# A macaron transformer block on one core: rotary halves swapped by DMA, probabilities normalised by ScalarE and VectorE instead of GpSimd

## The chip, the cores and the metric

The kernel runs on one core of one Trainium2 chip. The metric is the device time of one execution in microseconds. Engines are named as in the profile: PE is TensorE (PEld its weight loads), DVE VectorE, ACT ScalarE, POOL GpSimd, SP SyncE. M is used below for the moment at which DVE begins the row maxima of a pair of heads.

## The reference, cut to what matters

The input is 16 sequences of 256 tokens of width 256, in float32. The block is x + 0.5 ffn(layernorm(x)), then x + attention(layernorm(x)), then x + 0.5 ffn(layernorm(x)), with a ternary feed-forward layer of 1024 hidden columns. The change touches only the attention:

```python
q = (x @ Wq).reshape(b, n, 16, 128).transpose(0, 2, 1, 3)   # 16 heads; k and v have 4
k = (x @ Wk).reshape(b, n, 4, 128).transpose(0, 2, 1, 3)
q = q * cos + rotate_half(q) * sin                          # rotate_half: (-t2, t1)
k = k * cos + rotate_half(k) * sin
scores = einsum('bhid,bhjd->bhij', q, repeat(k, 4)) * scale, masked above the diagonal
attn = softmax(scores)
out = einsum('bhij,bhjd->bhid', attn, repeat(v, 4)) * head_scale
return out.reshape(b, n, 2048) @ Wo
```

## The kernel before

Every float32 operand of a matrix product is cut into a float16 high part and a float16 low part, and a product is three matmuls (high by high, high by low, low by high).

The program has three stages, one after the other: a feed-forward layer over 8 tiles of 512 tokens, the attention over 16 batches (sequences), and the second feed-forward layer. In the attention each engine runs the same loop: batches b, and in a batch 8 pairs of query heads, i from 0 to 7. One turn of the loop is called a slot here. Pair t = 8b + i passes through the slots with a fixed lag, so that in one slot an engine works on several pairs. Before the change, in the slot of pair t:

- PE projects the queries of pair t (in the slots i = 0 and i = 4 the keys of two key heads come first), makes the scores of pair t-2, the values product of pair t-5, and two heads of the output projection of the batch before. In the slots i = 3 and i = 7 it also projects values.
- ACT copies the two halves of the projected 128 x 512 tile, swapped, from PSUM to SBUF (`rope_swap`, L474, two copies of 64 partitions), takes the exponentials of pair t-2 (L502, four activations with row sums), casts the normalised probabilities of pair t-3 to float16 (L509), scales the output of pair t-5 (L518), and casts the rotated tile to float16 (L525, L528).
- DVE takes the row maxima of pair t-2 with the mask (L944, four operations on PSUM), multiplies the projection by the cosines (L925, from PSUM) and the swapped halves by the sines (L925, from SBUF), makes the low part of the output (L955), the reciprocals of the row sums (L960) and the low part of the probabilities of pair t-3 (L964, one operation of 768 columns with two SBUF inputs).
- POOL adds the two rotary products (`rope_add`, L339), multiplies the exponentials of pair t-2 by the reciprocals (`norm`, L358, four pieces of 128 or 256 columns) and makes the low part of the rotated tile (`rope_lo`, L343).
- SP issues one DMA transpose of the probabilities of a pair (L268), once their low part is there.

In the slots with keys (i = 0 and 4) there is a second rotary tile, so that a batch has 10 rotary tiles for 8 pairs. Each rotary tile uses one of two projection banks and one of two buffers. At the edge of a batch the finished rows of the batch two before are added, normalised and turned (L987, L992, L995, L1000, L1006 on DVE, L348 and L350 on POOL).

The order on each engine is that of the program text, and the engines are joined by counting semaphores. The waits around the change are: `rope_mul` of tile r waits for the swap of r and for the add of r-2 (two buffers); `rope_add` waits for `mul`; the cast to float16 waits for `add`; `rope_lo` waits for that cast; `scores` waits for `rope_lo`.

Of the kernel before, what the change touches and what calls it, by code (L numbers as in the profile page):

```python
# [23 lines left out]
F32 = mybir.dt.float32  # L24
# [28 lines left out]
def program(nc, x, wq, wk, wv, wo, hscale, wu, wg, wd, cos_t, sin_t, out):  # L53
    ctx = ExitStack()
    with ctx:
# [38 lines left out]
        def pieces(lo, hi, dt, b):  # L94
# [8 lines left out]
        M1, M2, QK = pieces(0, 1024, F32, 2), pieces(1024, 2048, F32, 2), pieces(2048, 3072, F32, 2)  # L103
# [9 lines left out]
        COS = sb("COS", [P, 256], F32)  # L113
        SIN = sb("SIN", [P, 256], F32)
# [29 lines left out]
        RI = sb("RI", [P, 2, 4], F32)  # L144

# [23 lines left out]
        proj, swap, mul, add, qk_hi, qk_lo, v_hi, v_lo = (  # L169
            sem(n) for n in ("proj_done", "rope_swapped", "rope_mul", "rope_add", "qk_hi", "qk_lo", "v_hi", "v_lo"))  # L170
        s_done, mx, ex, rcp, pn = (
            sem(n) for n in ("scores_done", "max_done", "exp_done", "recip_done", "probs_normed"))
# [79 lines left out]
        def _(sp):  # L252
# [14 lines left out]
            def turn_probs(par):  # L267
                sp.dma_start_transpose(PT[:, par, :, :], PR[:, par, :]).then_inc(pt_t[par], 16)  # L268

            for e in range(2):  # L270
                sp.wait_ge(p_lo, e + 1)
                turn_probs(e)
            with sp.Fori(1, STEPS // 2) as m:
                for par in range(2):
                    ready, used = sp.to_reg(2 * m + par + 1), sp.to_reg(2 * m + par - 1)
# [3 lines left out]
                    turn_probs(par)  # L279
# [12 lines left out]
        def _(gp):  # L292
# [59 lines left out]
            def norm(e, par):  # L352

                wait_alone(gp, rcp, e + 1)
                for hh in range(2):
                    for blk, (lo, hi) in enumerate(BLOCKS):
                        c, lo, hi = 2 * hh + blk, 384 * hh + lo, 384 * hh + hi
                        last = gp.tensor_scalar(EX[:, par, lo:hi], EX[:, par, lo:hi], RI[:, par, c:c + 1], PS, ALU.mult, ALU.mult)  # L358
                last.then_inc(pn, 1)

            def batch(b):
                for i in range(PAIRS):
                    g, k = divmod(i, 4)
                    u, t = 2 * b + g, PAIRS * b + i
                    r, m = 5 * u + 1 + k, (5 * g + 1 + k) % 2
                    if real(b, i, 0):
                        if k == 0:
                            if isinstance(b, int) and b + i == 0:
                                gp.wait_ge(ff[0]["down_done"], FC * TILES - 2)
                            rope_add(r - 1, 1 - m)  # L370
                        if isinstance(b, int) and b + i == 0:
                            gp.wait_ge(ff[0]["down_done"], FC * TILES)
                        rope_add(r, m)
                    if real(b, i, 2):
                        norm(t - 2, i % 2)
                    if real(b, i, 0):
                        if k == 0:
                            rope_lo(r - 1, 1 - m, KH[:, g, :], KL[:, g, :])
                        rope_lo(r, m, QH[:, i % 2, :], QL[:, i % 2, :])
# [23 lines left out]
        def _(act):  # L403
            act.dma_start(HS[:, :], hscale).then_inc(hs_in, 16)
            act.dma_start(COS[:, :], cos_t).then_inc(tab_in, 16)
            act.dma_start(SIN[:, :], sin_t).then_inc(tab_in, 16)

# [648 lines left out]
```

## Time and profile before

| what | value |
|---|---|
| median of 3 runs | 1285.54 us |
| lowest, highest run | 1285.26, 1293.14 us |
| the profiled execution | 1293.14 us, its span 1293.1 us |
| busy in the span: PE, DVE, ACT, POOL | 1102.5, 1028.9, 883.7, 916.3 us |
| probability transposes (one a pair) | 128, the first at 272.1 us, the last at 1110.9 us |

The profile is one execution, the one that took 1293.14 us. Its page gives the busy time of each engine, the span cut in 40 equal slices, the chain of work that ended last, and the groups of instructions by line. An instruction's duration overlaps its follower's by some hundredths of a microsecond, so that what an instruction takes of its engine's time is the distance from its start to the next start.

### The profile page before, as it was taken

The page shows a single profiled execution, that of the slowest core. Times are in us where ns is not written, and L with a number is a line of the kernel's source. Part 1 is how long each engine was busy: PE and PEld are TensorE (multiplying, and loading weights), DVE is VectorE, ACT ScalarE, POOL GpSimd, SP SyncE. Part 2 cuts the span into 40 slices and gives each one's busy share as a digit, 9 for nine tenths or more (in the row PEclk, how much of TensorE's full clock was granted, in tenths as well). Part 3 has the DMA queues.
Part 4 walks back from the last instruction along what each step waited for, and adds up shares of the span by engine and source line. Part 5 has one row for each costly group of instructions (what it writes and reads, how often), then busy time and mean ns, then how long its engine had stood idle before and what let it go on. Part 6 is the DMA issues. An engine that isn't in the chain of part 4 may idle for free.

```text
span 1293.1 us, 29339 instructions
## 1 busy us (share of the span) xinstructions
PE 1102.5 (85%) x9152; PEld 838.9 (65%) x9152; DVE 1028.9 (80%) x2398; ACT 883.7 (68%) x2155; POOL 916.3 (71%) x1048
## 2 busy tenths in 40 slices
PE   3588899968888988888898888978988888899998
PEld 1254455657676777767777777767777777655555
DVE  3587788588899999999999999999999999533333
ACT  3264556578777877878788787877878777454444
POOL 1643545578888888888888888888888888344443
PEclk9799899989999999999999999999999999999999
DMA  8110000013333333332333333233333323200000
GB/s 317 31 52 1 1 0 0 1 38 63 62 50 62 61 61 61 57 64 51 59 61 61 61 61 58 52 61 60 61 61 61 61 49 67 44 17 32 16 32 32
DMA packets 214034, 67.82 MB, mean 52 GB/s; under 512 B 201200, under 2 KB 212720, under 8 KB 213744
## 3 DMA queue, kind: packets, MB, share of 16 engines
q1 hardware_dynamic: 213568, 67.13, 24.6%
q8 instruction: 18, 0.29, 0.1%
q10 hardware_dynamic: 432, 0.27, 0.1%
q14 instruction: 16, 0.13, 0.0%
HBM read 12.85 MB, written 4.19 MB: 13 GB/s over the span
## 4 chain that ended last, share of the span: by engine, by line
POOL 34%; issue 22%; DVE 12%; PE 9%; ACT 3%; POOLq 1%; DMA 0%; DVEq 0%; ACTq 0%; SPq 0%
POOL SCR L358 10%; POOL SCR L343 9%; POOL SCR L339 9%; PE bank L599 9%; DVE SCR L925 5%; POOL SCR L322 5%; DVE bank L944 2%; ACT SCR L474 1%; DVE ARENA L955 1%; POOL VE L348 1%; DVE ARENA L964 1%; DVE NM L944 1%; ACT SCR L502 0%; DMA SCR<-ARENA 0%; PE bank L570 0%
## 5 line engine op out<-in xcount | busy, mean ns | idle before, releaser
L358 POOL TENSOR_SCALAR SCR<-SCR,RI 128x128 f32<-128x128 f32 (+1 forms) x512 | 274.8, 537 | 42.8 <-DVE RI L960 2.6
L322 POOL TENSOR_TENSOR SCR<-SCR 128x512 f16<-128x512 f32 x128 | 150.6, 1177 | 196.1 <-ACT SCR L425 189.3
L339 POOL TENSOR_TENSOR SCR<-SCR 128x512 f32<-128x512 f32 x160 | 217.3, 1358 | 74.3 <-DVE SCR L925 72.4
L502 ACT ACTIVATE SCR<-bank,NM 128x128 f32<-128x128 f32 (+1 forms) x512 | 208.1, 418 | 60.6 <-DVE NM L944 58.6
L599 PE MATMUL bank<-SCR 128*128 128x128 f16 (+1 forms) x1536 | 159.7, 255 | 89.2 <-POOL SCR L343 80.9
L343 POOL TENSOR_TENSOR SCR<-SCR 128x512 f16<-128x512 f32 x160 | 213.9, 1346 | 10.8 <-ACT SCR L528 0.7
L425 ACT CAST SCR<-SCR 128x512 f16<-128x512 f32 x128 | 79.1, 618 | 178.7 <-DVE SCR L800 126.3
L800 DVE SCALAR_TENSOR_TENSOR SCR<-SCR,CS,bank 128x512 f32<-128x512 f32 x128 | 95.2, 744 | 128.8 <-PE bank L570 88.2
L964 DVE TENSOR_TENSOR ARENA<-SCR,ARENA 128x768 f16<-128x768 f32 x128 | 189.6, 1482 | 9.6 <-ACT ARENA L509 9.5
L599 PE MATMUL bank<-WOH,ARENA 128*128 128x256 f16 x1024 | 192.5, 276 | 2.6 <-DVE X L987 1.4
L599 PEld LDWEIGHTS bank<-SCR 128*128 128x128 f16 x1536 | 115.6, 101 | 121.4 <-issue 81.3
L474 ACT COPY SCR<-bank 64x512 f32<-64x512 f32 x320 | 185.5, 580 | 6.6 <-PE bank L599 0.8
L944 DVE CUSTOM_DVE_ANT_0 bank<-bank,MASK,SCQ 128x128 f32<-128x128 f32 (+1 forms) x512 | 183.5, 417 | 4.5 <-PE bank L599 1.7
L925 DVE TENSOR_TENSOR SCR<-SCR,SIN 128x512 f32<-128x512 f32 x160 | 167.3, 1046 | 0.0
L599 PE MATMUL bank<-SCR,ARENA 128*128 128x256 f16 (+1 forms) x1536 | 160.9, 259 | 4.3 <-DMA SCR<-ARENA 2.3
L528 ACT CAST SCR<-SCR 128x512 f16<-128x512 f32 x128 | 80.1, 626 | 112.7 <-POOL SCR L339 110.3
L599 PEld LDWEIGHTS bank<-SCR,ARENA 128*128 128x128 f16 x1536 | 133.0, 103 | 33.4 <-issue 16.9
L588 PE MATMUL bank<-TD,SCR 128*128 128x256 f16 x1024 | 133.8, 275 | 18.3 <-DVE TD L859 11.9
L925 DVE TENSOR_TENSOR SCR<-bank,COS 128x512 f32<-128x512 f32 x160 | 109.6, 685 | 42.2 <-ACT SCR L474 40.9
L599 PE MATMUL bank<-WOL,ARENA 128*128 128x256 f16 x512 | 141.4, 276 | 0.0
L588 PEld LDWEIGHTS bank<-TD,SCR 128*128 128x128 f16 x1024 | 99.9, 98 | 59.7 <-POOL SCR L322 18.1
L599 PEld LDWEIGHTS bank<-WOH,ARENA 128*128 128x128 f16 x1024 | 101.9, 99 | 16.5 <-DVE ARENA L955 2.1
(118 smaller groups left out, 2151.8 us busy)
## 6 DMA issues: line engine op xcount, KB each, us to landing
out<-X SPq DMA_DIRECT2D x7, 512.0 KB, 2.9
X<-in_x SPq DMA_DIRECT2D x1, 2560.0 KB, 10.0
ARENA<-in_wq SPq DMA_DIRECT2D x1, 2048.0 KB, 13.0
ARENA<-in_wo SPq DMA_DIRECT2D x1, 2048.0 KB, 18.2
SCR<-ARENA SPq DMA_TRANSPOSE x128, 3.7
X<-in_x SPq DMA_DIRECT2D x3, 512.0 KB, 9.7
X<-in_wu SPq DMA_DIRECT2D x1, 1024.0 KB, 7.0
X<-in_wg SPq DMA_DIRECT2D x1, 1024.0 KB, 8.8
```

Of the source, the lines that this page charges most:

```text
L322: gp.tensor_tensor(HL[:, f % 4, :], H32[:, f % 2, :], HH[:, f % 4, :], ALU.subtract).then_inc(s["hl_done"], 1)
L339: gp.tensor_tensor(QK[:, m, :], M1[:, m, :], M2[:, m, :], ALU.add).then_inc(add, 1)
L343: gp.tensor_tensor(lo, QK[:, m, :], hi, ALU.subtract).then_inc(qk_lo, 1)
L358: last = gp.tensor_scalar(EX[:, par, lo:hi], EX[:, par, lo:hi], RI[:, par, c:c + 1], PS, ALU.mult, ALU.mult)
L474: last = act.copy(M2[d:d + 64, m, :], PJ[m][s:s + 64, :])
L502: last = act.activation(EX[:, par, 384 * hh + lo:384 * hh + hi], SBK[hh][:, lo:hi], ACT.Exp, bias=NM[:, par, c:c + 1], scale=-1.0, accum_o ...
L588: last = pe.matmul(YB[sub // 2][:, (sub % 2) * D:(sub % 2 + 1) * D], hs[:, f % 4, sub * P:(sub + 1) * P], TD[:, f, :], start=f == 0 and a ...
L599: last = pe.matmul(dst, l(c), r(c), start=start and x == 0, stop=stop and x == len(todo) - 1, skip_group_check=True)
L800: ve.scalar_tensor_tensor(H32[:, f % 2, :], SG[:, f % 2, :], CS[:, 0:1], GB[f % 2][:, :], ALU.mult, ALU.mult).then_inc(s["h_done"], 1)
L925: last = ve.tensor_tensor(two(dst), two(src), tb[:, :].unsqueeze(1).to_broadcast([P, 2, SEQ]), ALU.mult)
L944: last = ve.tensor_tensor_reduce(SBK[hh][:, lo:hi], SBK[hh][:, lo:hi], MASK[:, 256 - (hi - lo):256], SCQ[:, 0:1], 3e38, ALU.add, ALU.min, ...
L964: ve.tensor_tensor(PR[:, par, 768:1536], EX[:, par, :], PR[:, par, 0:768], ALU.subtract).then_inc(p_lo, 1)
```

## The change

The projection tile is read once from PSUM by one DVE multiplication of 1024 columns, which writes both products, tile by cosines and tile by signed sines, to SBUF (MM). SP then moves the two halves of the sine product into each other's place with two DMAs from SBUF to SBUF (64 partitions by 512 float32 columns each, into MS), behind the wait for `mul` and in one queue with the transposes. POOL adds MM and MS. The add, the cast and the low part of a rotary tile move one slot later on POOL and ACT. ACT's two copies go.

POOL's four normalising multiplications go. ACT writes the normalised high part itself in four pieces (`act.mul` with the reciprocal as scale), one slot later than POOL normalised, ahead of the exponentials. DVE makes the low part in four pieces too, each a multiply by the reciprocal (a column pointer) and a subtraction. The reciprocal is taken in two DVE steps (RI0, then a multiply by 4096 into RI), with the low part of the output between them, and the first of them now stands ahead of that low part. The sines' sign is moved in the host's table.

```diff
+            def swap_halves(r, m):
+                wait(sp, mul, r + 1)
+                for d, s in ((0, 64), (64, 0)):
+                    sp.dma_start(MS[d:d + 64, m, :], MM[s:s + 64, m, 1, :]).then_inc(swapped[m], 16)
+
+            def batch(b):                                   # SP
+                for i in range(PAIRS):
+                    g, k = divmod(i, 4)
+                    r, m = 10 * b + 5 * g + 1 + k, (5 * g + 1 + k) % 2
+                    if real(b, i, 0):
+                        if k == 0:
+                            swap_halves(r - 1, 1 - m)
+                        swap_halves(r, m)
+                    if real(b, i, 3):
+                        turn_probs(PAIRS * b + i - 3, (i - 3) % 2)
...
-            def rope_add(r, m):
+            def rope_add(r, m, nth):                        # POOL, one slot later
                 wait(gp, qk_lo, r - 1)
-                gp.wait_ge(mul, r + 1)
-                gp.tensor_tensor(QK[:, m, :], M1[:, m, :], M2[:, m, :], ALU.add).then_inc(add, 1)
+                gp.wait_ge(swapped[m], 32 * nth)
+                gp.tensor_tensor(QK[:, m, :], MM[:, m, 0, :], MS[:, m, :], ALU.add).then_inc(add, 1)
...
-            def norm(e, par):
-                wait_alone(gp, rcp, e + 1)
-                for hh in range(2):
-                    for blk, (lo, hi) in enumerate(BLOCKS):
-                        c, lo, hi = 2 * hh + blk, 384 * hh + lo, 384 * hh + hi
-                        last = gp.tensor_scalar(EX[:, par, lo:hi], EX[:, par, lo:hi], RI[:, par, c:c + 1], PS, ALU.mult, ALU.mult)
-                last.then_inc(pn, 1)
...
-            def rope_swap(r, m):                            # ACT
-                wait(act, add, r - 1)
-                for d, s in ((0, 64), (64, 0)):
-                    last = act.copy(M2[d:d + 64, m, :], PJ[m][s:s + 64, :])
-                last.then_inc(swap, 1)
...
+                    if real(b, i, 3):                       # ACT, ahead of the exponentials
+                        e, par = t - 3, (i - 3) % 2
+                        act.wait_ge(rcp, e + 1)
+                        wait(act, pt_t[par], 16 * (4 * b + (i - 3) // 2))
+                        for hh in range(2):
+                            for blk, (lo, hi) in enumerate(BLOCKS):
+                                c, cols = 2 * hh + blk, slice(384 * hh + lo, 384 * hh + hi)
+                                last = act.mul(PR[:, par, cols], EX[:, par, cols], RI[:, par, c:c + 1])
+                        last.then_inc(p_hi, 1)
...
+                    if real(b, i, 1):                       # ACT, straight behind the exponentials
...
+                        act.wait_ge(add, r + 1)
+                        wait(act, s_done, 2 * (t - 1) - 2)
+                        act.copy(QH[:, j % 2, :], QK[:, m, :]).then_inc(qk_hi, 1)
...
-                ve.wait_ge(swap, r + 1)                     # DVE, rope_mul
-                two = lambda a: a.rearrange("p (h n) -> p h n", h=2)
-                for dst, src, tb in ((M1[:, m, :], PJ[m][:, :], COS), (M2[:, m, :], M2[:, m, :], SIN)):
-                    last = ve.tensor_tensor(two(dst), two(src), tb[:, :].unsqueeze(1).to_broadcast([P, 2, SEQ]), ALU.mult)
-                last.then_inc(mul, 1)
+                ve.wait_ge(proj, done)
+                two = PJ[m][:, :].rearrange("p (h n) -> p h n", h=2)
+                ve.tensor_tensor(MM[:, m, :, :].rearrange("p k (h n) -> p k h n", h=2),
+                                 two.unsqueeze(1).to_broadcast([P, 2, 2, SEQ]),
+                                 CS_TAB[:, :, :].unsqueeze(2).to_broadcast([P, 2, 2, SEQ]), ALU.mult).then_inc(mul, 1)
...
+                    if real(b, i, 2):                       # DVE, behind rope_mul of pair t
+                        ve.wait_ge(ex, 2 * e + 2)
+                        ve.reciprocal(RI0[:, :], RS[:, par, :]).then_inc(rcp0, 1)
                     if real(b, i, 6):
...
                     if real(b, i, 2):
-                        ve.wait_ge(ex, 2 * e + 2)
-                        wait(ve, pn, e - 1)
-                        ve.reciprocal(RI[:, par, :], RS[:, par, :]).then_inc(rcp, 1)
+                        ve.wait_ge(rcp0, e + 1)
+                        ve.tensor_scalar(RI[:, par, :], RI0[:, :], PS, None, ALU.mult).then_inc(rcp, 1)
                     if real(b, i, 3):
                         ve.wait_ge(p_hi, t - 2)
-                        ve.tensor_tensor(PR[:, par, 768:1536], EX[:, par, :], PR[:, par, 0:768], ALU.subtract).then_inc(p_lo, 1)
+                        for hh in range(2):
+                            for blk, (lo, hi) in enumerate(BLOCKS):
+                                c, cols = 2 * hh + blk, slice(384 * hh + lo, 384 * hh + hi)
+                                last = ve.scalar_tensor_tensor(PR[:, par, 768 + cols.start:768 + cols.stop], EX[:, par, cols],
+                                                               RI[:, par, c:c + 1], PR[:, par, cols], ALU.mult, ALU.subtract)
+                        last.then_inc(p_lo, 1)
```

## Rows read from the trace of the kernel before

**Rows 1.** The page: busy time of each engine, then tenths by slice.
```profile
PE 1102.5 (85%) x9152; PEld 838.9 (65%) x9152; DVE 1028.9 (80%) x2398; ACT 883.7 (68%) x2155; POOL 916.3 (71%) x1048
...
DVE  3587788588899999999999999999999999533333
```

**Rows 2.** Windows: us; PE, PEld, DVE, ACT, POOL busy; clock; DMA share; GB/s.
```profile
600.00:700.00 100.00, 86.90 (x809) 73.28 (x807) 93.33 (x226) 79.25 (x214) 85.38 (x103) 0.95 0.31 59
```

**Rows 3.** Timeline, POOL: the same step of two batches, one after the other.
```profile
578.12 0.78 POOL L348 TENSOR_SCALAR VE<-MV 128x2 f32<-128x2 f32 x1
...
631.30 0.78 POOL L348 TENSOR_SCALAR VE<-MV 128x2 f32<-128x2 f32 x1
```

**Rows 4.** Timeline of one slot, 600.43 to 605.71 us, all engines: start, us.
```profile
600.43 0.34 DVE L944 CUSTOM_DVE_ANT_0 bank<-bank,MASK,SCQ 128x128 f32<-128x128 f32 x1
...
601.45 0.37 ACT L502 ACTIVATE SCR<-bank,NM 128x128 f32<-128x128 f32 x1
...
601.78 0.68 DVE L925 TENSOR_TENSOR SCR<-bank,COS 128x512 f32<-128x512 f32 x1
...
602.04 2.71 POOL L343 TENSOR_TENSOR SCR<-SCR 128x512 f16<-128x512 f32 x2
...
602.38 1.36 DVE L925 TENSOR_TENSOR SCR<-SCR,SIN 128x512 f32<-128x512 f32 x1
...
603.04 0.84 ACT L509 CAST ARENA<-SCR 128x768 f16<-128x768 f32 x1
603.67 0.68 DVE L955 SCALAR_TENSOR_TENSOR ARENA<-bank,ARENA 128x512 f16<-128x512 f32 x1
...
604.27 0.16 DVE L960 RECIPROCAL RI<-RS 128x4 f32<-128x4 f32 x1
604.35 1.22 DVE L964 TENSOR_TENSOR ARENA<-SCR,ARENA 128x768 f16<-128x768 f32 x1
...
605.71 0.36 DVE L944 CUSTOM_DVE_ANT_0 bank<-bank,MASK,SCQ 128x128 f32<-128x128 f32 x1
```

**Rows 5.** By line, 500 to 1000 us: count, busy us, mean ns, idle before.
```profile
L964 DVE TENSOR_TENSOR ARENA<-SCR,ARENA 128x768 f16<-128x768 f32 x75 | 113.3, 1511 | 3.7 <-ACT ARENA L509 3.7
L925 DVE TENSOR_TENSOR SCR<-SCR,SIN 128x512 f32<-128x512 f32 x94 | 99.9, 1063 | 0.0
L528 ACT CAST SCR<-SCR 128x512 f16<-128x512 f32 x76 | 47.6, 626 | 64.2 <-POOL SCR L339 61.8 <-PE bank L599 2.4
```

**Rows 6.** One line each: count, duration in ns (least/median/most).
```profile
L925 DVE TENSOR_TENSOR SCR<-bank,COS x160: 674/684/693, 251.7 to 1092.6; 128x512 f32<-128x512 f32 x160
L925 DVE TENSOR_TENSOR SCR<-SCR,SIN x160: 670/927/1668, 252.3 to 1093.2; 128x512 f32<-128x512 f32 x160
L964 DVE TENSOR_TENSOR ARENA<-SCR,ARENA x128: 957/1535/2006, 270.4 to 1109.9; 128x768 f16<-128x768 f32 x128
L339 POOL TENSOR_TENSOR SCR<-SCR x160: 1257/1268/2088, 253.3 to 1094.8; 128x512 f32<-128x512 f32 x160
L343 POOL TENSOR_TENSOR SCR<-SCR x160: 1147/1158/1708, 256.5 to 1098.8; 128x512 f16<-128x512 f32 x160
```

**Rows 7.** The nearest to the new pieces: a column pointer, 256 columns.
```profile
L845 DVE SCALAR_TENSOR_TENSOR WKL<-SCR,AFAC,WKH x4: 485/485/485, 146.1 to 219.4; - x4
...
618.79 0.86 DVE L987 SCALAR_TENSOR_TENSOR X<-bank,CW,X 128x256 f32 x2
```

**Rows 8.** Timeline, 221 us: four short DVE operations against one of POOL.
```profile
221.12 2.23 DVE L770 TENSOR_SCALAR SCR<-X,MV,RSTD 128x256 f32 x4 [0.61 <-POOL RSTD L309]
...
221.24 1.32 POOL L322 TENSOR_TENSOR SCR<-SCR 128x512 f16<-128x512 f32 x1 [0.24 <-ACT SCR L425]
```

**Rows 9.** DMA issues: count, KB each, median us from issue to landing.
```profile
SCR<-ARENA SPq DMA_TRANSPOSE x128, 3.7
...
out<-X SPq DMA_DIRECT2D x2, 256.0 KB, 2.2
COS<-in_cos_t ACTq DMA_DIRECT2D x1, 128.0 KB, 3.9
```

More of the change, by code:

```diff
@@ L101, in program @@
         XN = pieces(6144, 7168, F32, 4)
-        M1, M2, QK = pieces(0, 1024, F32, 2), pieces(1024, 2048, F32, 2), pieces(2048, 3072, F32, 2)
+        MM = SCR[:, 0:2048].rearrange("p (m k n) -> p m k n", m=2, k=2)
+        QK = pieces(2048, 3072, F32, 2)
+        MS = sb("MS", [P, 2, 512], F32)
         QH, QL = pieces(3072, 3584, F16, 2), pieces(3584, 4096, F16, 2)
@@ L167, in program @@
         half_done, out_done = sem("last_sums_half_done"), sem("out_done")
[L169 to L172, printed above, removed]
+        proj, mul, add, qk_hi, qk_lo, v_hi, v_lo = (
+            sem(n) for n in ("proj_done", "rope_mul", "rope_add", "qk_hi", "qk_lo", "v_hi", "v_lo"))
+        swapped = [sem(f"rope_swapped{i}") for i in range(2)]
+        s_done, mx, ex, rcp0, rcp = (
+            sem(n) for n in ("scores_done", "max_done", "exp_done", "recip_done", "recip_scaled"))
         pt_t = [sem(f"probs_turned{i}") for i in range(2)]
@@ L265, in _, with turn_probs @@
             sp.dma_start(XV[:, 12:32, :], xv[:, 12:32, :]).then_inc(xin[3], 16)
[L267 to L275, printed above, removed]
+            def swap_halves(r, m):
+                wait(sp, mul, r + 1)
+                for d, s in ((0, 64), (64, 0)):
+                    sp.dma_start(MS[d:d + 64, m, :], MM[s:s + 64, m, 1, :]).then_inc(swapped[m], 16)
+            def turn_probs(e, par):
+                if not isinstance(e, int):
+                    ready, used = sp.to_reg(e + 1), sp.to_reg(e - 1)
                     sp.wait_ge(consts, 5)
@@ L278, in _ @@
                     sp.wait_ge(o_done, used)
-                    turn_probs(par)
+                else:
+                    sp.wait_ge(p_lo, e + 1)
+                    wait(sp, o_done, e - 1)
+                sp.dma_start_transpose(PT[:, par, :, :], PR[:, par, :]).then_inc(pt_t[par], 16)
+            def batch(b):
[8 more added lines that the diff above has]
+                        turn_probs(PAIRS * b + i - 3, (i - 3) % 2)
+            batches(sp, batch)
             with sp.Fori(0, TILES - 1) as n:
@@ L504, in batch @@
                             last.then_inc(ex, 1)
[L505 to L509 removed]
+                    if real(b, i, 1):
+                        j, unit = (i - 1) % PAIRS, 2 * b + (i - 1) // 4
+                        gj, kj = divmod(j, 4)
+                        r, m = 5 * unit + 1 + kj, (5 * gj + 1 + kj) % 2
+                        if kj == 0:
+                            act.wait_ge(add, r)
+                            wait(act, s_done, 8 * unit - 8)
+                            act.copy(KH[:, gj, :], QK[:, 1 - m, :]).then_inc(qk_hi, 1)
+                        act.wait_ge(add, r + 1)
+                        wait(act, s_done, 2 * (t - 1) - 2)
+                        act.copy(QH[:, j % 2, :], QK[:, m, :]).then_inc(qk_hi, 1)
                     if k == 3 and real(b, i, 0):
@@ L935, in batch @@
                     if k == 0 and real(b, i, 0):
-                        rope_mul(r - 1, 1 - m)
+                        if isinstance(b, int) and b + i == 0:
+                            ve.wait_ge(ff[0]["h_done"], FC * TILES)
+                        rope_mul(r - 1, 1 - m, 6 * u + 1)
                     if real(b, i, 2):
```

66 lines of the change are left out of this document (21 added, 45 removed).

## The prediction

> **What bounds the kernel now.** I read the page first. PE has the highest mean, but the slices show DVE at nine tenths from the ninth to the thirty-fourth, the whole attention [rows 1]. A window inside it gives DVE 93%, PE 87%, POOL 85%, ACT 79% [rows 2], so DVE comes first there and the others have room. The same step of two successive batches stands 53.2 us apart [rows 3]; 16 batches of this are some 850 us of the span, and the two feed-forward stages, about 440 us, are not touched.
>
> The timeline of one slot shows what fills DVE [rows 4]. From start to start: maxima 1.35 us, cosine multiply 0.60, sine multiply 1.29, output low part 0.60, reciprocal 0.08, probability low part 1.36, in all 5.28. The cosine multiply reads PSUM and always takes 0.67 to 0.69 us. The sine multiply has the same size with both inputs in SBUF and takes 0.67 at best, 1.67 at worst; the probability low part 0.96 to 2.01 [rows 6]. Both wait for POOL: at 602.38 the sine multiply starts while POOL's first L343 runs, and ends where 0.6 us of work behind the end of that POOL operation puts it [rows 4]. So an operation of DVE with two SBUF inputs and one of POOL exclude each other. By mean less best, over 10 tiles and 8 pairs, that costs DVE 0.39 x 10 + 0.55 x 8 = 8.3 us of the 53.2 [rows 5, 6]. The longest wait beside it is ACT's for POOL's add, 62 us in 500 [rows 5].
>
> The question is therefore not how much work leaves POOL and ACT, but what is left on DVE and where POOL's operations now fall.
>
> **Removed and added on DVE.** An instruction takes its columns over 0.96 per ns plus 0.07 us of DVE's time (512 columns in 0.60 [rows 4]). The wide multiply has 1024 columns from PSUM; it isn't in the trace, and by that line it takes 1.07 + 0.07 = 1.13 us, with two multiplies (1.20) as its upper bound. It takes the place of 0.60 plus a sine multiply of mean 0.98 (1.063 less the overlap of 0.08): 10 x 0.45 = 4.5 us a batch saved. No PSUM operation here waits for POOL, so it should not either.
>
> The probability low part of 768 columns takes 0.88 us when free (0.957 less 0.08) and becomes four pieces with a column pointer. The nearest rows have 256 columns: two from PSUM span 0.86 us, so 0.39 from start to start, and one from SBUF lasts 0.485, so 0.40 [rows 7]. That is 0.13 over the columns; a piece of 128 then takes 0.26, and the four 1.30. Bounds: 1.07 if the pointer cost nothing, 1.6 for four of 256. I take 1.30. The second reciprocal step adds 0.08 (0.3 if it has to wait for POOL as the short operations of rows 8 do).
>
> Here stands a rule of the Trainium skill, "VectorE: DVE Perf Modes", in its section on the TRN2 errata: a VectorE operation on SBUF pays 58 cycles plus one per column, and many small tiles pay the fixed part each time. By it the four pieces take 1.04 us, 0.26 less than my rows give, which over 128 pairs would be 33 us less; the fixed part of 0.13 us in rows 7 speaks against it.
>
> Without any exclusion the DVE work of a batch would be 8 x (1.35 + 1.13 + 0.08 + 0.60 + 0.08 + 1.30) = 36.3, plus 2 key tiles (2.3), 2 value low parts of the size of L955 (1.2) and the rows of the finished batch (eight operations of 256 columns by the same line and two of a few columns, about 3.0): 42.8 us, ten below 53.2. That is the gain on offer. The same count for the kernel before is 39.5 us: the change adds 3 us of work to the busiest engine and must win it back from exclusion.
>
> **Where POOL's operations fall.** POOL loses its four normalising pieces and keeps, a batch, 10 adds of 1.26 us and 10 low parts of 1.16 [rows 6], about 25 us against 45 now. DVE's exposed stretch is what has two SBUF inputs: the second reciprocal step and the four pieces, 1.4 us a slot. I lay out a slot from M, the start of the maxima.
>
> In the slot of rows 4 ACT's first exponential starts 1.02 us behind M and the cast behind the last at 2.6. DVE: maxima to 1.35, wide multiply to 2.48. The first reciprocal now stands right behind it and waits for the exponentials, so it starts at about 2.7 (the wait of 0.2 us is new, 1.6 us a batch; before, the sine multiply and the output low part covered it). Then output low part to 3.38, and there the exposed stretch wants to begin. ACT's next work behind the exponentials is the cast L528 (0.62 us), whose input, the add, has long been made: its multiply ended 3.2 us before M, and with 3 us for the swap (below) the add runs to 1.1 behind M. So the cast ends at about 3.15, and POOL's low part L343 runs from 3.2 to 4.35. Both follow from the same event, the end of the exponentials, one by 0.6 to 0.65 us and the other by 0.7 to 0.8. The low part therefore meets the exposed stretch in every slot and costs it 0.95 us: the stretch runs from 4.33 to 5.71. A regular slot takes 5.7 us; 8 of them 45.6, with key tiles, value low parts and rows 52.1.
>
> If POOL comes second it is no better, because four pieces can be broken into: at 221 us four DVE operations of 0.4 us began 0.12 us before a POOL operation, which took 1.32 instead of 1.16, so it had the port after the first of them, and the four took 2.23 us together [rows 8]. The one operation of 768 columns could not be interrupted like that. So each POOL operation that arrives in the stretch costs its whole length. In the slots behind the key tiles POOL makes two low parts back to back: 2 x 1.16 = 2.3 more, 54.4. In the key slots the add of the key tile waits for the regular low part and starts right behind it, in the pieces: 2 x 1.26 = 2.5 at most, and I take half, 1.3: 55.7. The adds of the query tiles come at swap landing, about 5.5 behind M, at the last piece; they count nothing here, and up to 4.9 in the range where the stretch is already late.
>
> **The swap.** Two DMAs of 128 KB on SP, behind `mul` and ahead of the transpose. The nearest rows land in 2.2 us (256 KB) and 3.9 (128 KB at the start, beside the other loads); a transpose lands in 3.7 [rows 9]. With two issues of 0.4 I take 3 us behind the multiply, bounds 2.2 and 6. The DMA share is 0.31 [rows 2], so there is room. Nothing but SP's own queue stands behind the wait: a transpose has two slots until PE wants it, and `mul` of the next pair follows the low part that the transpose waits for, so SP gets no new blocking. The add is wanted by the end of the exponentials, 5.7 us behind the multiply; with 1.3 for the add itself the swap has 4.4 us before anyone waits, and every microsecond beyond that moves cast and low part back by as much.
>
> ACT loses two copies (1.17 us a tile) and the cast of 0.84, and gains four pieces of roughly 1.4 us; POOL loses 2 us a pair. Neither was first, so both count nothing, as long as DVE paces the slot. PE is busy 87% of 53.2, 46 us a batch [rows 2], and isn't the bound either.
>
> **The sum.** 55.7 - 53.2 = 2.5 us a batch, 16 batches: +40 us on the profiled 1293.1, so 1333. That execution was 7.6 us over the median of the runs, so 1326 for the median: +3%.
>
> **Rivals.**
> (a) The operations don't line up, and POOL's 25 us fall evenly over the batch. The stretch then meets a running operation with 0.45 x 0.6 = 0.27 us and is broken into by 0.37 a us x 1.0 us x 1.2 = 0.45: 0.7 a slot instead of 0.95 and no extra for the keys. 42.8 + 1.6 + 8 x 0.7 + 0.5 = 50.5, or 43 us less: 1243. For it: the sine multiply's duration now spreads from 0.67 to 1.67 us [rows 6], so the phases do vary. Against: the two releases by one event.
> (b) Nearly no exclusion, as the change intends: 42.8 + 1.6 and some waits, say 47: 1185. It decides if the low parts run under the maxima, that is if the add is late by more than 3 us. PE's 46 us a batch would come next.
> (c) A column pointer costs nothing in SBUF, so that the pieces take 1.07 us by the line above, and everything else is as forecast: 55.7 - 8 x 0.23 = 53.9, +11 us: 1296, within 1%. For it: the line holds for all other operations of rows 4. Against: both rows of rows 7. The errata section of the Trainium skill's page "VectorE: DVE Perf Modes" gives 1.04 us for them, and with it 1292.
> (d) Every add also falls in the stretch, because a longer stretch catches more of them: 54.4 + 2.5 + 4.9 = 61.8, +138 us: 1423. A swap of 6 us instead of 3 has the same effect, since the add then lands at 2.5 behind M and the low part in mid-stretch.
>
> **Chances.** Forecast 0.42 (1305 to 1365), (d) or its half 0.20, (a) 0.18, (b) 0.07, (c) 0.13. A difference within 1% (13 us) is about what a measurement of this kernel can't tell from none. Slower by over 1%: the forecast and (d), 0.62. Same: (c), 0.13. Faster: (a) and (b), 0.25. The range leaves out (b) and the far end of (d): 1240 to 1395. The forecast's own range is 1305 to 1365.
>
> **What the profile would show.** Each right if: the wide multiply is 1.21 us and never longer (else the PSUM argument fails); batches stand 55 to 57 us apart by L348's place; the pieces have least durations of 0.34 and 0.47 and means well above them, most of the excess in whichever piece comes as L343 begins; the second reciprocal step has a mean far over its least of 0.15; POOL is under 60% busy and DVE over 90%; the swaps land in about 2.5 us. A low part that starts under the maxima, or pieces at their least duration, would make me wrong towards faster; a POOL add that waits for the swap while ACT waits for the add, with DVE idle, would mean that the transfer sets the time, not the exclusion.

## The result, and the profile after

The changed kernel takes 1369.0 us against 1286.0 for the kernel before: ratio 1.064, interval 1.061 to 1.067. The prediction had the sign, and its range of 1240 to 1395 holds the time; the forecast was +40 us, and +83 were measured. The profiled execution has a span of 1368.4 us, 75 more than before.

The page of the changed kernel: busy time of each engine, then DVE's tenths by slice, then the new DMAs (KB each, median us to landing).
```profile
PE 1127.5 (82%) x9152; PEld 871.5 (64%) x9152; DVE 1142.0 (83%) x2750; ACT 787.4 (58%) x2219; POOL 597.3 (44%) x536
...
DVE  3585887799999999999999999999999999743333
...
MS<-SCR SPq DMA_DIRECT2D x320, 128.0 KB, 2.3
SCR<-ARENA SPq DMA_TRANSPOSE x128, 3.6
```
Its window for 600 to 700 us, columns as in [rows 2]:
```profile
600.00:700.00 100.00, 80.48 (x725) 68.80 (x724) 97.06 (x243) 62.30 (x203) 45.95 (x40) 0.90 0.48 98
```
POOL fell from 85% to 46% in this window and ACT from 79% to 62%, while DVE rose from 93% to 97% [rows 2]. Two engines were relieved, and the one that paces the attention was not. The clock granted to TensorE was 0.90 here and 0.95 before, but that does not set the time: between 500 and 1000 us DVE waits for PE 3.4 us in all, and the normalising half alone (below) takes the same time at a mean granted clock of 0.95, against 0.93 for the whole change.

The timeline of POOL, the same step of two successive batches, answers to [rows 3]:
```profile
600.71 0.19 POOL L367 TENSOR_SCALAR VE<-MV 128x2 f32<-128x2 f32 x1 [2.52 <-DVE MV L1003]
...
658.72 0.19 POOL L367 TENSOR_SCALAR VE<-MV 128x2 f32<-128x2 f32 x1 [2.53 <-DVE MV L1003]
```
A batch takes 58.0 us instead of 53.2. Sixteen times 4.8 is 77 us, so the whole difference arises in the attention.

One line each, as in [rows 6] (count, duration in ns least/median/most): the wide multiply, the two steps of the reciprocal, the four pieces of the probability low part, and POOL's low part.
```profile
L921 DVE TENSOR_TENSOR SCR<-bank,CS_TAB x160: 1201/1211/1226, 253.3 to 1167.4; 128x1024 f32<-128x1024 f32 x160
L955 DVE RECIPROCAL RI<-RS x128: 166/178/180, 266.6 to 1182.1; 128x4 f32<-128x4 f32 x128
L963 DVE TENSOR_SCALAR RI<-RI x128: 158/1058/1066, 266.8 to 1182.8; 128x4 f32<-128x4 f32 x128
L970 DVE SCALAR_TENSOR_TENSOR ARENA<-SCR,RI,ARENA x512: 335/471/1556, 272.0 to 1186.3; 128x128 f16<-128x128 f32 x86, 128x256 f16<-128x256 f32 x85
L362 POOL TENSOR_TENSOR SCR<-SCR x160: 1144/1154/1335, 260.3 to 1176.2; 128x512 f16<-128x512 f32 x160
```
The wide multiply never takes over 1.226 us: it reads PSUM, and once started it does not wait for POOL. The second step of the reciprocal works on four columns, has a least duration of 0.158 us and a median of 1.058. POOL's low part lasts 1.15 at the median and 1.34 at most, where it went up to 1.71 before [rows 6]: when this low part and DVE's four-column step meet now, it is DVE that waits.

How they meet is in the timeline of a regular slot, all engines, which answers to [rows 4]:
```profile
615.00 0.34 DVE L943 CUSTOM_DVE_ANT_0 bank<-bank,MASK,SCQ 128x128 f32<-128x128 f32 x1
...
616.34 1.21 DVE L921 TENSOR_TENSOR SCR<-bank,CS_TAB 128x1024 f32<-128x1024 f32 x1
...
617.43 0.63 ACT L515 CAST SCR<-SCR 128x512 f16<-128x512 f32 x1
617.58 1.10 SPq L274 DMA_DIRECT2D MS<-SCR  x2
617.58 0.18 DVE L955 RECIPROCAL RI<-RS 128x4 f32<-128x4 f32 x1
...
617.68 0.66 DVE L959 SCALAR_TENSOR_TENSOR ARENA<-bank,ARENA 128x512 f16<-128x512 f32 x1
...
618.14 1.16 POOL L362 TENSOR_TENSOR SCR<-SCR 128x512 f16<-128x512 f32 x1 [2.24 <-ACT SCR L515]
618.26 1.06 DVE L963 TENSOR_SCALAR RI<-RI 128x4 f32<-128x4 f32 x1
...
619.23 1.39 DVE L970 SCALAR_TENSOR_TENSOR ARENA<-SCR,RI,ARENA 128x128 f16<-128x128 f32 x4
...
620.46 1.30 POOL L358 TENSOR_TENSOR SCR<-SCR,MS 128x512 f32<-128x512 f32 x1 [1.17 <-DMA MS<-SCR]
620.55 0.68 DVE L975 SCALAR_TENSOR_TENSOR ARENA<-bank,ARENA 128x512 f16<-128x512 f32 x1
```
ACT's cast follows the last exponential and ends at 618.06. POOL's low part starts at 618.14, and 0.12 us later DVE comes to L963, which ends with the low part. The four pieces behind it then run in 1.32 us, as if free. From 615.00 to the end of the pieces at 620.55 are 5.55 us; 5.7 was forecast. The halves' DMAs are issued at 617.58, and the add (L358) starts at 620.46, 2.9 us behind the end of its multiply and within the last piece, which it no longer delays.

Then come the slots with a key tile. First POOL's timeline, then DVE's, which shows the four pieces as one row:
```profile
625.42 1.15 POOL L362 TENSOR_TENSOR SCR<-SCR 128x512 f16<-128x512 f32 x1 [3.66 <-ACT SCR L515]
626.53 2.54 POOL L358 TENSOR_TENSOR SCR<-SCR,MS 128x512 f32<-128x512 f32 x2
633.41 2.27 POOL L362 TENSOR_TENSOR SCR<-SCR 128x512 f16<-128x512 f32 x2 [4.34 <-ACT SCR L512]
635.80 1.54 POOL L358 TENSOR_TENSOR SCR<-SCR,MS 128x512 f32<-128x512 f32 x1
```
```profile
625.54 1.06 DVE L963 TENSOR_SCALAR RI<-RI 128x4 f32<-128x4 f32 x1
626.51 3.50 DVE L970 SCALAR_TENSOR_TENSOR ARENA<-SCR,RI,ARENA 128x128 f16<-128x128 f32 x4
...
634.51 3.38 DVE L970 SCALAR_TENSOR_TENSOR ARENA<-SCR,RI,ARENA 128x128 f16<-128x128 f32 x4
```
At 626.5 the adds of the key tile and of the query tile run back to back and both fall into the pieces: 3.50 us instead of 1.39. In the next slot, at 634.5, it is the second low part and, behind the second piece, a whole query add: 3.38. In the slot of 600.5 us two more things happen: POOL, which had waited 2.52 us for DVE's row statistics (the first row of the batch distance above), is so late with its add that the wide multiply waits for the buffer, and the next add runs into the centring of the row:
```profile
603.05 1.23 DVE L921 TENSOR_TENSOR SCR<-bank,CS_TAB 128x1024 f32<-128x1024 f32 x1 [1.04 <-POOL SCR L358]
...
605.21 2.38 DVE L970 SCALAR_TENSOR_TENSOR ARENA<-SCR,RI,ARENA 128x128 f16<-128x128 f32 x4
607.51 1.68 DVE L1008 TENSOR_SCALAR SCR<-X,MV,RSTD 128x256 f32 x2
```

### The profile page after: what moved, and what is told of

Read it like the earlier page. It is cut to its first block, busy times and chain, and to the rows that moved or that the text cites. A ratio compares the mean times of both kernels' runs of the same rounds, so it can differ in the third digit from the quotient of the medians.

```text
span 1368.4 us, 29292 instructions
## 1 busy us (share of the span) xinstructions
PE 1127.5 (82%) x9152; PEld 871.5 (64%) x9152; DVE 1142.0 (83%) x2750; ACT 787.4 (58%) x2219; POOL 597.3 (44%) x536
## 4 chain that ended last, share of the span: by engine, by line
issue 24%; PE 20%; POOL 17%; DVE 13%; ACT 4%; DMA 3%; SPq 1%; POOLq 1%; DVEq 0%; ACTq 0%
PE bank L597 19%; POOL SCR L358 6%; POOL SCR L362 6%; POOL SCR L341 4%; DVE ARENA L970 4%; ACT SCR L502 3%; DMA MS<-SCR 3%; DVE bank L943 2%; DVE RI L963 2%; DVE SCR L921 2%; DVE ARENA L959 1%; DVE NM L943 1%; SPq L274 1%; DVE ST L1000 0%; DVE SCR L1008 0%
## 5 line engine op out<-in xcount | busy, mean ns | idle before, releaser
L362 POOL TENSOR_TENSOR SCR<-SCR 128x512 f16<-128x512 f32 x160 | 183.5, 1155 | 381.8 <-ACT SCR L515 310.1
L970 DVE SCALAR_TENSOR_TENSOR ARENA<-SCR,RI,ARENA 128x128 f16<-128x128 f32 (+1 forms) x512 | 264.5, 574 | 0.0
L358 POOL TENSOR_TENSOR SCR<-SCR,MS 128x512 f32<-128x512 f32 x160 | 211.3, 1329 | 97.8 <-DMA MS<-SCR 92.3
L341 POOL TENSOR_TENSOR SCR<-SCR 128x512 f16<-128x512 f32 x128 | 150.7, 1178 | 201.5 <-ACT SCR L434 193.8
L493 ACT ACTIVATE ARENA<-SCR,RI 128x128 f16<-128x128 f32 (+1 forms) x512 | 191.0, 444 | 63.7 <-DVE RI L963 60.1
L921 DVE TENSOR_TENSOR SCR<-bank,CS_TAB 128x1024 f32<-128x1024 f32 x160 | 194.0, 1213 | 15.3 <-POOL SCR L358 14.8
L434 ACT CAST SCR<-SCR 128x512 f16<-128x512 f32 x128 | 79.1, 618 | 179.7 <-DVE SCR L798 126.8
L597 PE MATMUL bank<-SCR,ARENA 128*128 128x256 f16 (+1 forms) x1536 | 178.3, 276 | 0.7 <-DMA SCR<-ARENA 0.6
L963 DVE TENSOR_SCALAR RI<-RI 128x4 f32<-128x4 f32 x128 | 121.3, 947 | 0.1
L428 ACT ACTIVATE SCR<-bank,SU 128x512 f32<-128x512 f32 x128 | 87.6, 684 | 31.2 <-PE bank L560 29.9
L502 ACT ACTIVATION_READ_ACCUMULATOR SCR<-bank,NM 128x1 f32 x512 | 103.8, 203 | 0.0
```

Source lines behind the costliest of these rows:

```text
L341: gp.tensor_tensor(HL[:, f % 4, :], H32[:, f % 2, :], HH[:, f % 4, :], ALU.subtract).then_inc(s["hl_done"], 1)
L358: gp.tensor_tensor(QK[:, m, :], MM[:, m, 0, :], MS[:, m, :], ALU.add).then_inc(add, 1)
L362: gp.tensor_tensor(lo, QK[:, m, :], hi, ALU.subtract).then_inc(qk_lo, 1)
L493: last = act.mul(PR[:, par, cols], EX[:, par, cols], RI[:, par, c:c + 1])
L502: last = act.activation(EX[:, par, 384 * hh + lo:384 * hh + hi], SBK[hh][:, lo:hi], ACT.Exp, bias=NM[:, par, c:c + 1], scale=-1.0, accum_o ...
L597: last = pe.matmul(dst, l(c), r(c), start=start and x == 0, stop=stop and x == len(todo) - 1, skip_group_check=True)
```

## The experiments

The theory after the result: the probability low part, split into pieces and led by a four-column step, stands at a fixed distance behind the end of the exponentials, and so does POOL's low part; they meet in every slot, and since the pieces can be broken into, POOL's further operations get in too. The rivals were that the transfer of the halves delays POOL (rotary half of the change), and that the added work on DVE alone is the price. The kernel before took 1284.3 us beside the first four kernels and 1293 to 1296 beside the others, so only ratios are compared. To be explained: 1.064.

**One piece in place of four.**
```
-  for hh in range(2):
-      for blk, (lo, hi) in enumerate(BLOCKS): ...
-          last = ve.scalar_tensor_tensor(PR[...low], EX[...], RI[:, par, c:c + 1], PR[:, par, cols], ALU.mult, ALU.subtract)
+  ve.tensor_tensor(PR[:, par, 768:1536], EX[:, par, :], PR[:, par, 0:768], ALU.subtract).then_inc(p_lo, 1)
```


> The changed kernel, but the low part of the probabilities is again one tensor_tensor of 768 columns (EX minus the high part; the multiply by the reciprocal is left out of the low part). Exclusion theory: the slots lose the 0.42 us that four pieces cost over one (8 x 0.42 = 3.4 us a batch), and POOL can no longer come in between pieces, so that most of the extra 1.0 to 2.1 us of the slots behind the keys goes as well (about 5 us a batch): batches of 50 us instead of 58, 1369 - 16 x 8 = about 1240 us, range 1225 to 1270. Rival (the pieces cost only their own fixed part): 1369 - 55 = about 1315. Rival (the swap's latency or PE sets the slot): no less than 1350.

This kernel leaves out the multiply by the reciprocal in the low part. It takes 1295.3 us, ratio 1.009 (1.008 to 1.011). By line, 500 to 1000 us:
```profile
L963 DVE TENSOR_SCALAR RI<-RI 128x4 f32<-128x4 f32 x75 | 73.2, 977 | 0.0
L967 DVE TENSOR_TENSOR ARENA<-SCR,ARENA 128x768 f16<-128x768 f32 x75 | 71.9, 959 | 0.0
L943 DVE CUSTOM_DVE_ANT_0 bank<-bank,MASK,SCQ 128x128 f32<-128x128 f32 x150 | 53.0, 353 | 30.8 <-PE bank L597 29.1
```
The four-column step still waits for POOL in nearly every slot (mean 0.977), but the single operation has its least duration, 0.959, on average: once it holds its place, nothing gets in. The batches fall from 58.0 to between 53.0 and 54.2 us, 53.5 in the mean, and 5.5 of the 6.4 points are gone. The work saved is 1.32 less 0.88 (0.96 less the overlap) = 0.44 us a pair, or 3.5 a batch. What got in between the pieces goes as well: their means in the changed kernel were 597 and 538 ns, 262 and 68 over the least for their size, which makes 5.3 a batch. Of these 8.8 only 4.5 show, for others came back: the maxima now wait 3.1 us a batch for PE's scores (0.4 in the changed kernel), and the two centring operations of the rows take 1.26 us each (0.88). That is why the time lies above the 1225 to 1270 expected.

**No transfer** (the exchange of the halves is left out).
```
-  sp.dma_start(MS[d:d + 64, m, :], MM[s:s + 64, m, 1, :]) ...   # and its calls
-  gp.wait_ge(swapped[m], 32 * nth); gp.tensor_tensor(QK[:, m, :], MM[:, m, 0, :], MS[:, m, :], ALU.add)
+  gp.wait_ge(mul, r + 1);           gp.tensor_tensor(QK[:, m, :], MM[:, m, 0, :], MM[:, m, 1, :], ALU.add)
```


> The changed kernel without the two swap DMAs; POOL adds the two products straight behind the multiply (the exchange of the halves is left out). Exclusion theory: the transfer is hidden, but the adds come about 3 us earlier, under the output low part and the exposed stretch: 1.0 us behind the multiply instead of 3, so they may meet the stretch in every slot; 1350 to 1440 us, not faster by more than 20 us. Rival (the transfer's latency is what made it slower): clearly faster, 1290 to 1320.

1430.9 us, ratio 1.115 (1.113 to 1.117): without its DMAs the kernel is 5 points slower. POOL's timeline, DVE's pieces in the same slot, and the pieces by line, 500 to 1000 us:
```profile
632.34 1.15 POOL L358 TENSOR_TENSOR SCR<-SCR 128x512 f16<-128x512 f32 x1 [4.66 <-ACT SCR L511]
633.45 1.27 POOL L354 TENSOR_TENSOR SCR<-SCR 128x512 f32<-128x512 f32 x1
```
```profile
633.43 2.49 DVE L966 SCALAR_TENSOR_TENSOR ARENA<-SCR,RI,ARENA 128x128 f16<-128x128 f32 x4
```
```profile
L966 DVE SCALAR_TENSOR_TENSOR ARENA<-SCR,RI,ARENA 128x128 f16<-128x128 f32 x130 | 104.6, 805 | 0.0
...
L966 DVE SCALAR_TENSOR_TENSOR ARENA<-SCR,RI,ARENA 128x256 f16<-128x256 f32 x130 | 86.8, 667 | 0.0
```
Without the wait for the landing, the add (L354 here) follows the low part (L358) back to back and falls into the pieces, which take 2.49 us here instead of 1.39. In the changed kernel the means were 597 and 538 (window 500 to 1000 us), so the pieces of an average slot take 0.67 us more; 128 slots of that are 86 us, of which 62 show in the time. That is rival (d) of the prediction, in the slots that the changed kernel had spared. The transfer was hidden, and its delay kept the query adds out of the pieces.

**The rotary half alone** (GpSimd normalises, as before, between its adds and its low part; one low part operation of 768 columns on DVE) and **the other half alone** (kernel before, with the normalising of the changed one):
```
rotary half, GpSimd:   add, add | + norm(PAIRS * b + i - 2, i % 2) | rope_lo, rope_lo
other half:            COS / SIN tables, rope_swap on ACT and two multiplies as before;
                       ACT's four act.mul, reciprocal in two steps and DVE's four pieces as in the change
```


> The rotary half of the change alone; POOL normalises as before, one low-part operation. Exclusion theory: POOL's work is as before (about 39 us a batch free of waits) and DVE loses its sine multiply with two SBUF inputs, 10 x 0.6; port time of both together falls from 39 + 14 = 53 us to 39 + 8 = 47 a batch, and DVE needs 40: 48 to 50 us a batch, 1200 to 1240 us. Rival (the transfers cost more than the copies they replace): 1285 or more.

> The normalising half alone, on the kernel before: pieces on ACT and DVE, rotary part by copies and two multiplies. Exclusion theory: DVE has 43.5 us a batch free of waits, and both the sine multiply and the interruptible stretch of 1.4 us a slot meet POOL's adds and low parts: 55 to 60 us a batch, 1310 to 1390 us. Rival (taking the four pieces off POOL is the gain, the rotary half the loss): 1200 to 1260 us.

The normalising half alone takes 1369.0 us, ratio 1.066 (1.064 to 1.068), the same as the whole change, with a batch of 57.9 us. It meets POOL at other places: the sine multiply is free (mean 675 ns), and the pieces wait.
```profile
L963 DVE SCALAR_TENSOR_TENSOR ARENA<-SCR,RI,ARENA 128x256 f16<-128x256 f32 x138 | 128.4, 930 | 0.0
```
The rotary half alone takes 1561.8, ratio 1.217 (1.215 to 1.219). That is far over the 1200 to 1240 expected, and falls among the "1285 or more" of the rival, the transfers, but the next run shows another cause. The waits of the rotary half, 500 to 1000 us (total, times, longest):
```profile
DVE bank L951 <- PE bank L605: 185.9, 58, 5.3
POOL SCR L377 <- DVE RI L969: 167.9, 57, 3.8
...
PE bank L605 <- POOL SCR L362: 137.3, 52, 3.6
```
It is a ring. POOL's normalising (L377) waits for DVE's reciprocal, the rotary low part (L362) stands behind it, PE's scores wait for that low part, and DVE's maxima wait for the scores. I put the normalising on the wrong side of the low part. The repair is to move it behind, and ACT's cast with it:
```
 rope_add; rope_add
-norm(PAIRS * b + i - 2, i % 2)
 rope_lo; rope_lo
+norm(PAIRS * b + i - 2, i % 2)
```


> The rotary half alone again, but POOL makes the low part of the rotated tile ahead of the normalising pieces instead of behind them, and ACT casts the rotated tile ahead of the probabilities. If the 1562 us came from a ring (low part behind normalising behind the reciprocal behind the exponentials, and the next scores behind the low part), it opens: 1200 to 1290 us. If the transfers or their waits made it slow, it stays above 1450.

1313.5 us, ratio 1.014 (1.012 to 1.017). The ring is open, with the transfers as they were, so 20 of the 22 points were the order. But 0.93 to 1.00 times the time before was not reached, and a part for the transfers is not excluded. In 500 us, DVE waits 56 for ACT's cast and PE 85 for the rotary low part; POOL is busy 79%. Why it isn't faster I have read only in part. So the rotary half, at this order, brings nothing by itself; its 0.45 us saved per multiply do not show.

**The low part of the query tiles cut to 64 of 512 columns.**
```
-  gp.tensor_tensor(lo, QK[:, m, :], hi, ALU.subtract) ...
+  gp.tensor_tensor(lo[:, 0:n], QK[:, m, 0:n], hi[:, 0:n], ALU.subtract) ...   # n: 64 for query tiles, 512 for key tiles
```


> The changed kernel, but POOL's low part of the query tiles has 64 of its 512 columns (the rest of the low parts is left out), so that it holds the port for about 0.2 us instead of 1.16. Exclusion theory: the scaled reciprocal no longer waits (its mean falls from 0.98 us to under 0.35), each slot gets 0.8 us shorter and the second low part behind the keys goes: about 8 us a batch, 1369 - 130 = 1240 us; where PE's wait for the low part sets the pace the floor is about 1200. Rival (pieces cost by their number, not by who holds the port): over 1340.

1217.9 us, ratio 0.940 (0.938 to 0.942), 12 points better for taking 0.85 us off an operation of an engine that is busy 46%. By line:
```profile
L970 DVE SCALAR_TENSOR_TENSOR ARENA<-SCR,RI,ARENA 128x256 f16<-128x256 f32 x165 | 78.1, 473 | 0.0
L970 DVE SCALAR_TENSOR_TENSOR ARENA<-SCR,RI,ARENA 128x128 f16<-128x128 f32 x164 | 69.4, 423 | 0.0
L963 DVE TENSOR_SCALAR RI<-RI 128x4 f32<-128x4 f32 x82 | 27.2, 332 | 0.0
L362 POOL TENSOR_TENSOR SCR<-SCR 128x64 f16<-128x64 f32 x82 | 25.2, 308 | 138.6 <-ACT SCR L515 138.6
```
The four-column step goes from 0.978 to 0.332, and the pieces of 256 to their free duration. By the means that is 0.65 us a slot for the step and 0.48 for the pieces, in all 9.0 a batch, and the two centring operations give 0.9 more (401 ns each instead of 876). The batches fell to between 48.0 and 49.4 us, by 9.6 in the mean. So POOL's low part costs DVE more than its own length (8 x 0.85 = 6.8).

**The second reciprocal step given to ACT.**
```
+act.wait_ge(rcp0, e + 1)
+act.mul(RI[:, par, :], RI0[:, :], PS).then_inc(rcp, 1)
-ve.tensor_scalar(RI[:, par, :], RI0[:, :], PS, None, ALU.mult).then_inc(rcp, 1)
```


> The changed kernel, but ACT makes the scaled reciprocal instead of DVE. It waited 0.9 us for the port in every slot. Exclusion theory: the first piece waits in its place and only the instruction's own 0.08 us goes, 10 us in all: 1350 to 1369. Rival (a short operation in the port's queue is a cost of its own, 128 x 0.9): 1255 to 1290.

1347.6 us, ratio 1.040 (1.037 to 1.042). With nothing in front of it, the first piece waits instead: the pieces of 128 columns have a mean of 842 ns (597 in the changed kernel) and those of 256 a mean of 651 (538). That gives back 0.7 of the 0.9 us a slot that the step had taken; the time is a little under the 1350 to 1369 expected. Most of the wait belongs to the place in the slot, not to the instruction.

**All the work, but one low part operation.** ACT normalises into the f32 buffer, then casts, so DVE can subtract at once:
```
-last = act.mul(PR[:, par, cols], EX[:, par, cols], RI[:, par, c:c + 1])      # last.then_inc(p_hi, 1)
+last = act.mul(EX[:, par, cols], EX[:, par, cols], RI[:, par, c:c + 1])      # last.then_inc(pn, 1)
+act.wait_ge(pn, e + 1)
+act.copy(PR[:, par, 0:768], EX[:, par, :]).then_inc(p_hi, 1)
-four ve.scalar_tensor_tensor
+ve.tensor_tensor(PR[:, par, 768:1536], EX[:, par, :], PR[:, par, 0:768], ALU.subtract).then_inc(p_lo, 1)
```


> The changed kernel, but ACT normalises in float32 in place (four pieces) and casts to float16 in a fifth operation, so that DVE's low part is one subtraction of 768 columns again. ACT gains 0.85 us a slot and was at 63%. Exclusion theory: the same time as with one piece, 1295 us (1285 to 1310), since ACT isn't the bound. Rival (ACT's chain from the reciprocal to the high part is near critical): 1330 or more.

1312.1 us, ratio 1.012 (1.010 to 1.014), batches of 54.0 to 55.1 us, the operation at a mean of 945 ns. It confirms the first experiment with nothing left out: four pieces cost 5 points more than one operation.

**DVE's order changed, so that the pieces stand ahead of the end of the exponentials.**
```
DVE, a slot:  maxima, multiply, reciprocal, output low part, RI step, pieces
becomes:      multiply, maxima, pieces(t-3), reciprocal, output low part      # RI step on ACT
```


> All the work of the changed kernel, DVE's slot in another order: multiply of pair t, maxima of pair t-2, the four pieces of pair t-3, first reciprocal, output low part; the scaled reciprocal on ACT. By the lay-out of a slot the stretch with two SBUF inputs now lies 2.5 to 3.8 us behind the slot's start, POOL's add at 4.1 and its low part at 4.4 or later, so they no longer meet. Exclusion by place in the slot: 48 to 50 us a batch, ratio to the kernel before 0.93 to 0.96. Rival (what counts is the amount of port time, or the number of pieces, wherever they stand): at least the 1.04 of the kernel with the reciprocal on ACT.

1335.7 us, ratio 1.032 (1.030 to 1.035); 0.93 to 0.96 was expected. By line, and the largest wait of PE:
```profile
L961 DVE SCALAR_TENSOR_TENSOR ARENA<-SCR,RI,ARENA 128x256 f16<-128x256 f32 x142 | 67.8, 477 | 0.0
L961 DVE SCALAR_TENSOR_TENSOR ARENA<-SCR,RI,ARENA 128x128 f16<-128x128 f32 x142 | 49.0, 345 | 0.0
```
```profile
PE bank L599 <- POOL SCR L362: 85.3, 36, 4.5
```
The pieces are almost at their least durations, as laid out. But DVE is now busy only 80%. The rotary low part is released at the end of ACT's exponentials, PE's scores wait up to 4.5 us for it, and in 500 us DVE then waits 31.4 for PE's projection, 18.3 for its scores and 34.3 for POOL's adds. The exclusion was removed and a ring through PE took its place. So I moved ACT's rotary cast ahead of the exponentials, which lets POOL start while DVE is at the maxima:
```
+QH / KH casts of pair t-1
 exponentials of pair t-2
-QH / KH casts of pair t-1
```


> As reorder, and ACT casts the rotated tile of pair t-1 ahead of the exponentials of pair t-2 instead of behind them, so that POOL's low part runs from about 1.6 to 2.8 us behind the slot's start, under the maxima, and PE gets it 2.7 us earlier. If the ring through PE (low part, scores, maxima, exponentials, cast) sets reorder's pace: faster than reorder by 1 to 3%, ratio 0.91 to 0.94. If the add isn't there in time, ACT waits for it ahead of the exponentials and it is slower than reorder.

> As reorder, with ACT normalising in float32 in place and casting (the low part one subtraction). If the pieces no longer meet POOL, one subtraction saves DVE only 0.42 us a slot and costs ACT 0.85: within 2% of reorder. If they still meet it, clearly faster than reorder.

> reorder_hi_first, with ACT normalising in float32 in place and casting, so that DVE's low part is one subtraction that POOL can't break into. In reorder_hi_first the pieces still lasted 0.51 and 0.66 us against 0.34 and 0.47 when free, so exclusion still cost DVE about 0.7 us a slot, and one subtraction saves 0.42 more. If DVE sets the pace there: ratio 0.93 to 0.96. If ACT does (73% busy, 0.85 us a slot more work, all of it ahead of the exponentials): at least 0.975.

| kernel | time, us | ratio (interval) | mean batch, us |
|---|---|---|---|
| new order | 1335.7 | 1.032 (1.030 to 1.035) | 56.3 |
| new order, one low part operation | 1337.3 | 1.033 (1.031 to 1.036) | 56.3 |
| new order, cast first | 1259.4 | 0.973 (0.970 to 0.975) | 51.2 |
| both | 1216.0 | 0.940 (0.937 to 0.942) | 48.5 |

The cast moved ahead brings 6 points, so the ring was what held the new order back; 0.91 to 0.94 had been expected, and in row 3 the pieces meet POOL again (means 509 and 660 ns). One operation instead of four is worth nothing in rows 1 and 2, where the pieces meet no POOL operation, and 3.3 points in rows 3 and 4, where they do. In rows 1 and 2 DVE isn't the bound, though, so the work saved would not show there in any case. The last kernel does the whole computation, is 6% faster than the kernel before and 12% faster than the changed one. Its window from 500 to 1000 us, its low part and the first reciprocal step:
```profile
sum 500.00, PE 454.30 PEld 401.48 DVE 426.69 ACT 450.32 POOL 283.93; mean PE 454.30 PEld 401.48 DVE 426.69 ACT 450.32 POOL 283.93
```
```profile
L960 DVE TENSOR_TENSOR ARENA<-SCR,ARENA 128x768 f16<-128x768 f32 x83 | 90.8, 1094 | 0.0
...
L963 DVE RECIPROCAL RI<-RS 128x4 f32<-128x4 f32 x83 | 14.6, 176 | 44.4 <-ACT SCR L517 43.4
```
PE is at 91%, ACT at 90%, DVE at 85%. DVE no longer paces alone, since it waits 43 us in 500 for ACT's exponentials. PE has the most work, as rival (b) said of a kernel without exclusion, but PE waits 44 us for the rotary low part, so that it sets the time is not shown.

## Why the prediction was right or wrong

**Right.** DVE paces the attention, and the change adds work to it that it had to win back. The wide multiply costs 1.21 and never more. The phases: the end of the exponentials releases both low parts, the rotary one meets the exposed stretch in every slot, and the slot takes 5.55 us (forecast 5.7; the wait of 0.2 us for the exponentials, in front of the reciprocal, is not there). Four free pieces take 1.40 - 0.08 = 1.32 us in the reordered kernel (forecast 1.30); the errata section of the Trainium skill's "VectorE: DVE Perf Modes" gives 1.04, which the trace does not bear out, and so rival (c) is out. The pieces are broken into. Swaps land in 2.3 us (forecast 2.5) and hide. What ACT and POOL were spared did not make the kernel faster. Rivals (a) and (b) did not occur in the changed kernel. That the range holds the time is no merit of the sum: the range was drawn wide for (a) and (d).

On the exclusion itself the Trainium skill ("SBUF — State Buffer", section "SBUF: two separate sides") says that the shared port pair is an exclusive lock, held by whoever starts first for the whole instruction, and that a VectorE operation takes it if it has two SBUF inputs or runs in a two-port mode (L963, with one input, would be the latter). The trace agrees as to the instruction (L963 ends with POOL's), and adds that between back-to-back pieces the lock changes hands: 3.50 us for 1.32 us of work.

**The step that failed** is the adds: "2 x 1.26 = 2.5 at most, and I take half, 1.3" for the key tiles, and "they count nothing here" for the query tiles. The sum had 1.3 us a batch for them, and they took about 5.1. The batch, term by term:

| term, us a batch | forecast | measured |
|---|---|---|
| 8 slots, key tiles, value low parts, rows | 52.1 | 44.4 + 2.3 + 1.2 + 3.2 = 51.1 |
| second low part behind the keys | 2.3 | about 2.0 |
| adds | 1.3 | about 5.1 |
| rest | 0 | about -0.2 |
| sum | 55.7 | 58.0 |

The 5.1 are read from the rows above: 2.1 in the slot of 622 us (3.43 from start to start, less 1.32), where the key add and the query add both fall in the pieces; 1.0 in the next one (3.31 from start to start, less 1.32, less 1.0 for the second low part); 1.0 that the wide multiply waits for the buffer of the late add; 0.9 in the centring of the row (1.60 from start to start, against 0.68 for two free operations of 256 columns by the prediction's line). The centring lost as much in the kernel before (mean 877 ns each, 876 here), so it is missing in the prediction's sum but is no part of the change. The rest is a wait of 0.4 for PE's scores at 643.8, less 0.6 where the four-column step lasted only 0.44, at 604.9. The split is read from one batch; the sum is the distance of its two ends. The slots came out 1.0 under their forecast, which hid a part of what the adds had over.

I had the mechanism, and it stood in my rival (d), "every add also falls in the stretch, because a longer stretch catches more of them". But I placed the adds by the regular slot. In a key slot the stretch is longer by the first add or the second low part, and the query add, which comes some 3 us behind its multiply there as in the regular slot (624.84 to 627.76), meets it. A stretch that grows by what falls into it cannot be costed at its first length. Rival (d) for the key slots alone, with both key adds whole and one query add beside each, would have been 52.1 + 2.3 + 2.5 + 2.5 = 59.4, against 58.0 measured.

Left open: why the rotary half, once its ring is open, is 1.4% slower than before and not faster; and in the first experiment the saved work (3.5 us a batch) and the break-ins (5.3) are told apart by the rows alone, not by a run of its own.

## What to carry to other kernels

Moving work off a half-idle engine saves nothing; ask what remains on the engine that paces, and with which operations of the other side of an exclusion each of its operations is released. Several short operations in place of one long one cost more than their fixed parts where another engine can get in between them, and every operation so let in makes room for the next. When the order is changed to part two engines, follow each result through all engines back to its source before running it: the two kernels of the new order with the cast behind lost to a ring what they had won from exclusion, and the rotary half alone lost 20 points to one.

## What the runs showed of the hardware

- A multiply by a constant of 128x4 f32 on DVE waits for GpSimd (158/1058/1066 ns). A reciprocal of the same size, also from SBUF to SBUF, does not: in [rows 4] it starts at 604.27, inside POOL's low parts (602.04 to 604.75), and takes 0.16 us, and none of the 128 of that kernel took over 0.18. I had expected at most 0.3 us for the multiply's wait.
- Back-to-back DVE instructions let a waiting GpSimd operation in between: four pieces took 3.50 us against 1.40 undisturbed, with two adds of 1.27 inside.
- The exclusion works in both directions, on short operations too. GpSimd's two-column step of the rows takes 0.19 us here and took 0.78 before [rows 3]. There it began at 578.12 and ended at 578.90, just behind the probability low part of DVE, which has two SBUF inputs and ran from 577.71 to 578.85. Where the step followed GpSimd's own pieces without that operation beside it, in the rotary half with its ring open, it took 0.19.
- A transfer of 128 KB from SBUF to SBUF over 64 partitions lands 2.3 us from its issue (2.2 to 3.7), while transposes run on the same queue.
